# Cross-attention values turned by VectorE in 32 by 32 blocks and laid in place by eight small DMAs per sequence, in place of TensorE products and a VectorE copy

## The reference, cut to what matters

```python
q = (layer_norm(x) @ Wq)                       # [112, 16 heads, 64]
k, v = split(layer_norm(context) @ Wkv)        # [375, 64] each
s = q @ k.T * 64 ** -0.5 + mask                # [16 x 112, 375]
attn = softmax(s)
out = (attn @ v) @ Wout                        # v is needed with its 375 rows across partitions
```

## Time and profile before

| | us |
|---|---|
| median of three runs | 1895.42 |
| the profiled execution | 1893.93 |
| its span, first to last instruction | 1892.1 |
| TensorE busy | 1783.0 (94%) |
| VectorE busy | 1302.0 (69%) |
| ScalarE busy | 927.1 (49%) |
| GpSimd busy | 420.1 (22%), all but one instruction before the attention part |
| mean granted TensorE clock | 0.981 of full speed |

### The profile page before, as it was taken

The page is one execution under the profiler, slowest core; times in us unless marked ns, Lnnn a source line. Parts: engine busy times, 40 slices in busy tenths (PEclk is TensorE's granted clock), DMA queues, the critical chain, the costliest instruction groups (busy, mean ns, idle before and its releaser), DMA issues.

```text
span 1892.1 us, 27875 instructions
## 1 busy us (share of the span) xinstructions
PE 1783.0 (94%) x9320; PEld 1035.3 (55%) x9320; DVE 1302.0 (69%) x3970; ACT 927.1 (49%) x2262; POOL 420.1 (22%) x569
## 2 busy tenths in 40 slices
PE   4579999999999999999999999999999999999997
PEld 2346666666667544455445554545545545555466
DVE  6888988988957587476567557657737656755743
ACT  3353563463441456446445545545645644554542
POOL 4866876876861010000000000000000000000000
PEclk8789999999999999999999999999999999999999
DMA  4000001001014242232222222222222222222200
GB/s 129 11 10 21 11 21 30 11 21 31 1 38 148 59 152 73 51 75 73 63 64 67 72 70 58 59 66 79 58 63 76 74 59 63 70 60 70 54 13 20
DMA packets 75181, 106.13 MB, mean 56 GB/s; under 512 B 11456, under 2 KB 68736, under 8 KB 74144
## 3 DMA queue, kind: packets, MB, share of 16 engines
q1 hardware_dynamic: 74576, 103.90, 20.2%
q10 hardware_dynamic: 464, 0.46, 0.1%
HBM read 96.92 MB, written 7.42 MB: 55 GB/s over the span
## 4 chain that ended last, share of the span: by engine, by line
PE 76%; DVE 17%; DMA 2%; issue 2%; ACT 1%; POOL 1%; SPq 0%; DVEq 0%; POOLq 0%; ACTq 0%
PE ps L1500 20%; PE ps L1455 9%; PE ps L1462 9%; PE ps L1493 9%; PE ps L1478 8%; DVE m_u L725 3%; PE ps L404 3%; PE ps L388 3%; PE ps L314 2%; DVE m_rs L757 2%; PE ps L1560 2%; PE ps L439 2%; PE ps L1600 1%; PE ps L1554 1%; PE ps L424 1%
## 5 line engine op out<-in xcount | busy, mean ns | idle before, releaser
L1839 DVE CUSTOM_DVE_ANT_0 x_pr<-ps,x_mk 128x375 f32<-128x375 f32 x448 | 227.6, 545 | 312.1 <-issue 200.0
L1711 ACT ACTIVATE x_pT<-ps 125x384 f32<-125x384 f32 x448 | 195.4, 489 | 269.2 <-PE ps L1462 268.2
L1717 ACT ACTIVATE x_pr<-x_pr,x_mx 128x375 f32<-128x375 f32 x448 | 268.2, 608 | 34.5 <-DVE x_mx L1839 34.4
L1462 PEld LDWEIGHTS ps<-ident,x_pr 128*125 128x125 f32 x1344 | 163.6, 187 | 129.2 <-issue 91.2
L1455 PE MATMUL ps<-x_kT,x_qT 64*128 64x375 f32 x896 | 204.0, 530 | 23.7 <-DVE x_mx L1839 17.7
L1462 PE MATMUL ps<-ident,x_pr 128*125 128x128 f32 x1344 | 206.0, 290 | 0.0
L1500 PE MATMUL ps<-x_xn,x_w 128*128 128x448 f32 x512 | 203.8, 541 | 0.0
L1848 DVE TENSOR_SCALAR x_pr<-x_pr,x_rc 128x375 f32<-128x375 f32 x448 | 169.4, 421 | 8.0
L1478 PE MATMUL ps<-x_pT,x_va 125*64 125x512 f32 (+1 forms) x768 | 160.2, 553 | 0.6 <-ACT x_pT L1711 0.6
L314 PE MATMUL ps<-m_xa,w_in 128*128 128x448 f32 x352 | 145.1, 563 | 6.2 <-ACT m_xa L530 6.2
L1455 PEld LDWEIGHTS ps<-x_kT,x_qT 64*128 64x128 f32 x896 | 68.7, 186 | 144.0 <-issue 115.4
(11 more groups left out here) (196 smaller groups left out, 2880.8 us busy)
## 6 DMA issues: line engine op xcount, KB each, us to landing
x_mk<-in_mask SPq DMA_DIRECT2D x224, 187.5 KB, 2.4
x_cx<-in_context SPq DMA_DIRECT2D x32, 375.0 KB
x_cT<-in_context_turned SPq DMA_DIRECT2D x32, 375.0 KB, 3.2
x_rb<-context_roots SPq DMA_DIRECT2D x32, 187.5 KB, 5.1
m_Rd<-bc_roots SPq DMA_DIRECT2D x8, 448.0 KB, 3.4
x_mixed<-m_x SPq DMA_DIRECT2D x8, 448.0 KB, 3.7
X<-x_mixed SPq DMA_DIRECT2D x8, 448.0 KB, 3.8
m_X<-in_x SPq DMA_DIRECT2D x7, 448.0 KB, 4.0
```

Source lines behind the costliest of these rows:

```text
L1462: last = pe.transpose(bank(2 + e)[0:JP, t * ROWS:(t + 1) * ROWS], pr[:, 2 * (p % SLOT) + e, t * JP:(t + 1) * JP], ident[:, :])
L1711: act.activation(pT[:, 2 * NV * (batch(p) % 2) + 2 * (p % NP % NV) + e, :, :].rearrange("p t s -> p (t s)"), bank(2 + e)[0:JP, 0:JT * ROWS ...
L1717: act.activation(pr[:, k, :], pr[:, k, :], ACT.Exp, scale=-1.0, bias=mx[:, k:k + 1], accum_out=sums[:, k:k + 1]).then_inc(h_e.sem, 1)
L1839: dve.tensor_tensor_reduce(pr[:, k + e, :], bank(e)[:, 0:J], mk[:, p % SLOT, :], -1.0, 3.0e38, ALU.add, ALU.min, mx[:, k + e:k + e + 1]).t ...
```

## The change

The `vback` piece is gone: from the table, from `START`, from the seats, and from TensorE's and VectorE's programs. In its place, right behind the bias in the `kv` piece, VectorE waits for its own result and transposes `vT` from partitions 64 to 127 into partitions 0 to 63, block by block of 32 by 32 (one instruction over 64 x 384; the three padding columns of each tile of 128 are cleared once). SyncE, at the step where `vback` stood, waits for that transpose and issues eight DMAs from SBUF to SBUF, which put every block where it belongs in `va`. Six of them move 32 partitions x 3 tiles x 32 floats, two move 29 x 3 x 32. VectorE's next transpose and `times_v` wait for the DMAs' semaphores.

```diff
     for b in range(GB):
-        for r, kind in ((NP - 2, "kv"), (NP - 1, "vback")):
-            at[(b - 1) % GB * NP + r, "X"].insert(0, (kind, b))
+        at[(b - 1) % GB * NP + NP - 2, "X"].insert(0, ("kv", b))
...
+        def values_in(i, b):
+            sp.wait_ge(c_t.sem, c_t.value(i, b + 1))
+            hold(sp, h_o, i, NB * (b - 1))
+            for k in range(DH // 32):
+                for q in range(ROWS // 32):
+                    n = min(32, JP - 32 * q)
+                    sp.dma_start(va[32 * q:32 * q + n, b % 2, :, 32 * k:32 * k + 32], vT[32 * k:32 * k + n, :, 32 * q:32 * q + 32]).then_inc(l_va[b % 2].sem, 16)
...
                 if r == 3:
                     roots_in(g, n)
+                if r == NP - 1:
+                    values_in(g, n)
...
             if r == NV - 1:
-                emptied(pe, made_in(i, b), ("vback", b))
+                pe.wait_ge(l_va[b % 2].sem, l_va[b % 2].value(i, VPARTS * 16 * (b // 2 + 1)))
...
-            elif kind == "vback":
-                pe.wait_ge(c_v.sem, c_v.value(held_by(it, n), n + 1))
-                to, done = vacant(pe, it, piece)
-                for t in range(JT):
-                    last = pe.transpose(to[0:JP, t * DH:(t + 1) * DH], vT[DH:2 * DH, t * JP:(t + 1) * JP], ident[DH:2 * DH, DH:2 * DH])
-                last.then_inc(done, 1)
...
-                dve.tensor_scalar(vT[DH:2 * DH, :], src[DH:2 * DH, 0:J], kvb[DH:2 * DH, :], None, ALU.add).then_inc(c_v.sem, 1)
-            elif kind == "vback":
-                src, done = filled(dve, it, piece)
-                hold(dve, h_o, held_by(it, n), NB * (n - 1))
-                dve.tensor_copy(va[:, n % 2, :, :], src[0:JP, 0:JT * DH].rearrange("p (t d) -> p t d", d=DH)).then_inc(done, 1)
+                dve.tensor_scalar(vT[DH:2 * DH, :, 0:JP], src[DH:2 * DH, 0:J].rearrange("p (t q) -> p t q", q=JP), kvb[DH:2 * DH, :], None, ALU.add).then_inc(c_v.sem, 1)
+                dve.wait_ge(c_v.sem, c_v.value(held_by(it, n), n + 1))
+                last = n - 1 if n > 0 else GB - 1
+                if held_by(it, n) > 0 or n > 0:
+                    at = held_by(it, n) if n > 0 else held_by(it, n) - 1
+                    dve.wait_ge(l_va[last % 2].sem, l_va[last % 2].value(at, VPARTS * 16 * (last // 2 + 1)))
+                dve.transpose(vT[0:DH, :, :].rearrange("p t q -> p (t q)"), vT[DH:2 * DH, :, :].rearrange("p t q -> p (t q)")).then_inc(c_t.sem, 1)
```

More of the change, by code:

```diff
@@ L1051 @@
 CONTEXT = (0, 1, 4)
+VPARTS = DH // 32 * (ROWS // 32)
 CROOT = 2 * JT + 1 + RSQRT
@@ L1086 @@
 START = [("token", 0), ("token", 1), ("mlp", 0), ("mlp", 1), ("query", 0), ("mlp", 2), ("query", 1), ("mlp", 3), ("query", 2),
-         ("mlp", 4), ("query", 3), ("mlp", 5), ("query", 4), ("mlp", 6), ("kv", 0), ("query", 5), ("mlp", 7), ("query", 6), ("vback", 0),
-         ("query", 7)]
+         ("mlp", 4), ("query", 3), ("mlp", 5), ("query", 4), ("mlp", 6), ("kv", 0), ("query", 5), ("mlp", 7), ("query", 6), ("query", 7)]
 AHEAD = [piece for piece in START if piece[0] != "mlp"]
@@ L1100, in seat @@
         return 2
-    if piece[0] in ("kv", "vback"):
-        return 2 if piece[1] != 1 else int(piece[0] == "vback")
+    if piece[0] == "kv":
+        return 2 if piece[1] != 1 else 0
     return piece[-1] % 2
@@ L1188, in attention @@
     kT = sb("x_kT", [128, 2, J])
-    vT = sb("x_vT", [128, J])
+    vT = sb("x_vT", [128, JT, ROWS])
     va = sb("x_va", [JP, 2, JT, DH])
@@ L1228, in attention @@
     l_ct = count("x_lct", 16 * GB)
+    l_va = [count(f"x_lva{n}", VPARTS * 16 * GB // 2) for n in range(2)]
+    c_t = count("c_t", GB)
     l_rs = count("x_lrs", 16 * GB)
@@ L1428, in sync @@
         tokens_out(LAST - 2)
+        values_in(0, 0)
         group(0, first=True)
@@ L1588, in end_out @@
                 emptied(pe, NG - 1, ("value", KH - 1))
-                emptied(pe, NG - 1, ("vback", 3))
+                emptied(pe, NG - 1, ("kv", 3))
             elif h == 1 and k0 == 0:
@@ L1905, in part @@
                 src, _ = filled(dve, it, piece)
-                if it >= 0:
-                    filled(dve, it if n != 1 else it - 1, ("vback", (n - 1) % GB))
-                dve.tensor_scalar(vT[DH:2 * DH, :], src[DH:2 * DH, 0:J], kvb[DH:2 * DH, :], None, ALU.add).then_inc(c_v.sem, 1)
-            elif kind == "vback":
-                src, done = filled(dve, it, piece)
-                hold(dve, h_o, held_by(it, n), NB * (n - 1))
-                dve.tensor_copy(va[:, n % 2, :, :], src[0:JP, 0:JT * DH].rearrange("p (t d) -> p t d", d=DH)).then_inc(done, 1)
+                dve.tensor_scalar(vT[DH:2 * DH, :, 0:JP], src[DH:2 * DH, 0:J].rearrange("p (t q) -> p t q", q=JP), kvb[DH:2 * DH, :], None, ALU.add).then_inc(c_v.sem, 1)
[5 more added lines that the diff above has]
+                dve.transpose(vT[0:DH, :, :].rearrange("p t q -> p (t q)"), vT[DH:2 * DH, :, :].rearrange("p t q -> p (t q)")).then_inc(c_t.sem, 1)
             elif kind == "back":
@@ L1995, in group @@
                     final_norm(it - 1, FINAL.index(p))
+        dve.memset(vT[DH:2 * DH, :, JP:ROWS], 0.0)
         dve.sem_inc(f_s.sem, f_s.first)
@@ L2008, in vector @@
         part(-1, ("kv", 0))
-        part(-1, ("vback", 0))
         group(0, first=True)
```

## The result

The changed kernel takes 1875.26 us (median of four runs, 1873.88 to 1875.91), the kernel before 1895.87 us beside it. The ratio is 0.9891 with a 95% interval of 0.9874 to 0.9908. The forecast was 1875.5 us. The span of the profiled execution went from 1892.1 to 1871.7 us, 20.4 us less, where the sum had 19.8.

The account below looks back on a forecast made before the run. TensorE was taken to bound the kernel. Dropping 30 counted vback pieces at 0.66 us saves 19.8 us, 1893.93 to 1874.1; with 1.5 us to the median 1875.6, stated as 1875.5 us, range 1870 to 1887.

Parts of the forecast that it names:

- the sum: Whole kernel: 30 x 0.66 = 19.8 us saved, so 1893.93 - 19.8 = 1874.1 us for the profiled execution.
- What bounds: TensorE bounds the kernel, busy 98.6% between 900 and 1800 us; removed work counts fully unless its neighbours then wait.
- 0.66 us for each of 30: TensorE's vback in steady steps, steps 13 and 27 of group 0 and the prologue: 0.47 + 0.19 us each, 19.8 us.
- The 0.19 us in the row behind: TensorE's eight products after vback take 3.21 us instead of 3.01, as short products do not cover the next weight load.
- Two at nothing: The vbacks at steps 6 and 20 of group 0, where no output pieces follow, were counted as saving nothing.
- The transpose: VectorE's new 64 x 384 transpose: 0.55 us plus 0.05 wait, cost 0; rival of 1.9 us gives 1884.5 us, chance 0.09.
- The queue and the engines: SyncE's eight issues, some 3 us, and 218 packets of 15 ns (3.3 us) on one engine per sequence: cost 0.
- The danger: Rival: one DMA engine chokes and roots come late from 94 ns per packet; 1915 us at 100 ns, chance 0.09.
- 20.4 against 19.8: The forecast side is 19.8 us: 30 vback pieces at 0.66 us each on TensorE.

Follow-up runs that it names:

- that run: Changed kernel with each 32-row transfer cut into one of 31 rows and one of 1 row, meant for one DMA engine: 1877.30 us, ratio 0.9893.

## Why the prediction was right

**What bounds.** Confirmed: the two runs that leave out the products or the added work both end at the changed kernel's time, and at its steady group of 152.04 us. (The scores' waits of the earlier trace rows are spread over 224 steps, 8 groups of 28, and not over 448; nothing else rests on that.)

**0.66 us for each of 30.** Confirmed in size, 2.65 us for four in a steady group; the last group, with three, is 1.91 us shorter. The 0.19 us in the row behind was the part that a sum of busy times would have missed. What each product is worth was not what an even split gives (0.107 us and not 0.157).

**Two at nothing.** At step 6 of group 0 the maximum follows the scores as before. The timeline of the changed kernel there:

```profile
658.19 0.90 PE L1467 MATMUL ps<-x_kT,x_qT 64*128 64x375 f32 x4
...
659.22 0.55 DVE L1845 CUSTOM_DVE_ANT_0 x_pr<-ps,x_mk 128x375 f32<-128x375 f32 x1 [1.56 <-issue]
```

It starts 1.03 us behind them, as in the earlier trace rows. For step 20 the length of group 0 answers: it is 2.77 us shorter, and the two that count (1.3 us) and the clock (1.6 us, below) make that up, with nothing left for steps 6 and 20.

**The transpose.** 0.573 us against 0.55 taken. It hid at step 12 as said. At step 27 ScalarE's first query copy now has no idle time before it, but TensorE never waits for it.

**The queue and the engines.** The issues took twice what I read from neighbouring rows, 0.62 us each at the median instead of 0.28 to 0.35. A packet: the queue's share went from 20.2% to 22.1%, and (0.221 x 1871.7 - 0.202 x 1892.1) x 16 us / 27136 = 18.5 ns. That difference, from which the forecasts of the experiments take their 18 ns, is not a packet's price. The run without the small transfers has a share of 20.9%, so the time of the other packets alone moves by 9 us, a third of the difference, from one execution to another. A short window inside one transfer of 29 rows is cleaner. Changed kernel, 1095.9 to 1096.5 us, packets, MB, share:

```profile
q1 hardware_dynamic: 64, 0.01, 8.7%
```

0.087 x 16 x 0.6 us / 64 = 13 ns is the length of a packet's record, where 15 were taken; and 64 packets in 0.6 us are one every 9.4 ns, since the records overlap. So a transfer of 29 rows holds its engine for 88 x 9.4 ns = 0.83 us, and 218 packets are about 2 us and not 3.3. The danger was further off than the prediction had it. And 848 packets are 6 x (96 + 16) + 2 x (87 + 1): the transfers of 29 rows did run on one engine each, if each engine adds one completion packet. By the rule of the Trainium skill, "DMA: Bandwidth & Descriptors", section "Why a DMA increments its semaphore by 16 and not by 1" (the largest number of engines up to 16 that divides the slowest dimension longer than 1 on both sides), that number is what comes out, and the trace agrees. It also gives three engines for the transfers of a single row with three tiles, as the packets of that run show.

**20.4 against 19.8.** Six steady groups give 15.9 us and the rest is group 0 and the ends, where two things that the change does not touch differ between the two executions. In group 0 TensorE's clock was granted at 0.72 on average (a mix of its two levels, 1.2 and 2.4 GHz) for 6.1 us in the kernel before, and at 1.00 in the same place after. Windows, before and after:

```profile
630.50:636.60 6.10, 6.08 (x22) 3.85 (x22) 5.51 (x30) 2.12 (x8) 0.00 (x0) 0.72 0.46 127
```

```profile
631.00:635.50 4.50, 4.50 (x22) 3.08 (x22) 4.08 (x23) 1.50 (x7) 0.00 (x0) 1.00 0.46 132
```

The same 22 products took 1.6 us less. The mixer ended about 1 us later. They nearly cancel; that the median came within 0.3 us of the forecast is partly luck, since a single execution of the kernel lies up to 1.4 us from the median. Of the 30 pieces the one in the prologue, ahead of group 0, can't be checked because of the mixer's shift.

## What to carry to other kernels

Where TensorE follows TensorE through the chain of waits, price a small piece by the chain with and without it, the row behind it included, not by its busy time. Where a stage repeats, compare its length in the traces: here it repeats to 0.02 us in most groups, while whole times differ by several us. Work moved to another engine is free only up to the first place where that engine hands something on: find that place and its room before moving more. A transfer that is read seven steps later may be slow and badly shaped, but it shares its queue with others that are not; there the tightest reader counts, and it is in the first, thin group rather than in the steady ones.

## What the runs showed of the hardware that was not expected

An issue of a small SBUF to SBUF transfer of three dimensions takes twice as long as one of a mask or of the roots, 0.62 us against 0.28 to 0.35. All of them in the changed kernel (ns: least, median, most):

```profile
L1366 SPq DMA_DIRECT2D x_va<-x_vT x256: 586/624/1905, 623.3 to 1779.0; - x128
```

Packets of 128 bytes on one engine follow one another every 9.4 ns, as worked out above.

A short wait of TensorE can cost more than itself. Windows of the run with transfers one step before use: the stretch ahead of the wait, the wait, the twelve products behind it, and the stretch after (the clock is the third number from the right).

```profile
1180.00:1185.07 5.07, 5.07 (x31) 3.02 (x30) 4.93 (x17) 4.83 (x15) 0.00 (x0) 1.00 0.21 48
1185.08:1188.40 3.32, 0.00 (x0) 0.01 (x1) 0.00 (x0) 1.01 (x3) 0.00 (x0) 0.96 0.23 41
1188.42:1192.75 4.33, 4.33 (x13) 1.31 (x13) 4.01 (x16) 0.00 (x0) 0.00 (x0) 0.64 0.24 68
1193.00:1200.00 7.00, 7.00 (x29) 3.78 (x28) 2.40 (x9) 5.51 (x16) 0.00 (x0) 1.00 0.06 7
```

Behind 3.3 us without products the granted clock is 0.64 on average for 4.3 us, a mix of 2.4 and 1.2 GHz, and then 1.00 again: 1.6 us lost on top of 3.35. Groups 2 to 5 all show it. Group 1 does not: behind a wait of 3.39 us its twelve products take 2.79 us at full clock, and the group is 1.2 to 1.3 us shorter than those four:

```profile
875.69:878.50 2.81, 2.81 (x13) 0.97 (x13) 2.74 (x10) 0.00 (x0) 0.00 (x0) 1.00 0.19 47
```

What decides between the two is not shown by these runs.
